# TensorE repeats an unread product at three of its waits in a gated attention and mixture-of-experts kernel

## The chip, the cores and the metric

The kernel runs on one core of one Trainium2 chip. The metric is the device time of one execution in microseconds (us). Below, TensorE is PE in the profile, VectorE is DVE, ScalarE is ACT, GpSimd is POOL, SyncE is SP; PEld is the loading of weights into TensorE's array, which is listed apart from its matmuls.

## What is computed

Input x is 8 batches of 512 tokens of 128 features, all f32. With `xn` the layer norm of x:

```
s = attention(xn)      # 8 heads of 16; out1 - lam * out2; layer norm; times Wo, plus bo
g = silu(ffn(xn))      # 8 experts of width 512; every token goes to experts h and h+1, h from its first two features
out = x + s * g
```

The attention applies a softmax over 512 keys in each of 64 head-and-batch pairs. Each expert is `relu(x @ W1 + b1) @ W2 + b2`, and the two experts of a token are averaged.

## The kernel before, in words

**The schedule.** Function `schedule` (L76) gives every step of the work a due time by hand and sorts the steps. Each engine then runs through the same sorted list and issues its own share of every step, so the order of steps on each engine is fixed when the program is built; semaphores hold an engine until what it needs is there. The step kinds that matter here are `invert`, `turn_tile`, `hidden`, `turn_o`, `turn_z`, `project_o` and `finish`.

**The routing.** VectorE finds for each token which slot of which expert's tiles it takes (`route`, L692 to L764). It and GpSimd then build 32 one-hot matrices `at_row` (`find_rows`, L381 to L386), in four groups of eight; groups 2 and 3 are GpSimd's (`POOL_ROWS`). TensorE's step `invert` (L1084 to L1096) waits for `token_ready` (L756) and then, group by group, for the matrices, and sums 32 products into one bank of PSUM: the token number of every slot. VectorE turns that into the indices `inverse` (L902 to L904). GpSimd then gathers the 128 rows of the first expert tile with an indirect DMA (`load_tile`, L537), and SP loads that tile's pair of experts' weights (L462).

**An expert tile.** There are 39. For each, TensorE transposes the gathered rows (`turn_tile`, L1097 to L1101), VectorE copies them out (L921), TensorE multiplies by the two experts' W1 (`hidden`, L1110), ScalarE and VectorE apply the bias and the maximum (L647, L928), TensorE multiplies by both W2 (`down`, L1125), VectorE adds a bias (L937) and GpSimd scatters the result (L571). Before the first tile's transpose TensorE's list has the first five scores and the transposes of batch 1 (L982); behind it come two scores, the first half of `hidden` of tile 0, a score, and a projection of batch 1 (L996).

**Attention.** For each of 256 blocks of 128 queries by 512 keys TensorE makes scores (L1015), VectorE takes their row maximum (L822), TensorE makes them again with the maximum subtracted (L1044, 24 blocks later), ScalarE takes the exponential (L628) and TensorE multiplies by the values (L1056). After two groups of 16 blocks a batch is turned (`turn_o`, L1064), normed on VectorE and GpSimd (L869 to L880 and L560 to L563), turned again (`turn_z`, L1066 to L1071), multiplied by Wo (`project_o`, L1076) and given its bias (L889).

**The end.** The last batch's `turn_o`, norm, `turn_z` and `project_o` come one after the other, with nothing else left in TensorE's list. Beside them VectorE and GpSimd do the `finish` of the batches (L378 and L379: times the gate, plus x), and SP stores the results.

**PSUM.** There are eight banks: two for scores, two for `exp_bank`, one for the product with the values, three in a ring. `exp_bank[0]` is first written when the 24th block of attention is due, and is no longer read once the last exponential is taken.

Of the kernel before, what the change touches and what calls it, by code (L numbers as in the profile page):

```python
# [11 lines left out]
P = 128  # L12
# [53 lines left out]
DVE_FINISH = tuple(b for b in range(B) if b not in POOL_FINISH)  # L66
FINISH_AT = (8.1, 8.2, 12.1, 12.2, 14.5, 8.1, 8.2, 18)
ROW_GROUPS = 4
RING = 3
DRAIN = NT * HEADS - LAG  # L70
WB = 3
# [71 lines left out]
def gated_attention_moe(nc, x, wq, bq, wk, bk, wv, bv, wo, bo, lq1, lk1, lq2, lk2,  # L143
# [19 lines left out]
    with ctx:  # L163
# [779 lines left out]
        def _(pe):  # L943
# [8 lines left out]
            for s, use in uses.items():  # L952
# [16 lines left out]
                    "hidden": lambda: (hid_ready[s[2]], s[1] + 1),  # L969
                }[kind]()  # L970

            w2_of = {}
            pe.wait_ge(consts_ready, 1)
            for s in steps:
# [32 lines left out]
                elif kind == "score":  # L1007
                    n = s[1]
                    b, col = divmod(n, HEADS * C)
                    hh, c = divmod(col, C)  # L1010
                    if col == 0:
                        pe.wait_ge(stacked[b % STK], 12 * 16 * (b // STK + 1))
                    if n >= 2:
                        pe.wait_ge(max_taken, n - 1)
                    t.matmul(score_bank[n % 2][:, :], qs[0:MAX_ROW, b % STK, hh, c * P:(c + 1) * P],  # L1015
                             ks[0:MAX_ROW, b % STK, hh, :], start=True, stop=True).then_inc(score_filled, 1)
                elif kind == "turn_max":
                    grp = s[1]
                    pe.wait_ge(max_split, grp + 1)
                    free(uses[s])  # L1020
                    t.transpose(shared[0:PARTS * 16, 0:P // 2].bitcast(BF16),
                                max_parts[:, grp % 2, :, :].rearrange("p j n -> p (j n)"),
                                ident_bf[:, :]).then_inc(shared_filled, 1)
                elif kind == "b1":
                    pe.wait_ge(b1_loaded, 16)
                    free(uses[s])
                    t.transpose(shared[:, 0:EXP * FC], b1_rows[:, :], ident[0:EXP * FC, 0:EXP * FC]).then_inc(shared_filled, 1)
                elif kind == "exp":
                    n = s[1]
                    b, r = divmod(n, HEADS * C)  # L1030
                    g2, r = divmod(r, C * HALF)
                    kc, i = divmod(r, HALF)
                    hh = g2 * HALF + i
                    if n % 16 == 0:
                        pe.wait_ge(max_stacked, 16 * (n // 16 + 1))
                        if n == 0:
                            pe.wait_ge(ones_stacked, 16 * STK)
                    if n >= DRAIN + 4:
                        pe.wait_ge(exp_done, n - 3)
                    elif n >= DRAIN + 2:  # L1040
                        pe.wait_ge(max_taken, n - DRAIN + NT * HEADS - 3)
                    elif n >= 2:
                        pe.wait_ge(exp_done, n - 1)
                    t.matmul(exp_banks[n][:, :], ks[0:KROWS, b % STK, hh, kc * P:(kc + 1) * P],  # L1044
                             qs[0:KROWS, b % STK, hh, :], start=True, stop=True).then_inc(exp_filled, 1)
                elif kind == "pv":
                    n4 = s[1]
                    grp, kc = divmod(n4, C)
                    b = grp // 2
                    pe.wait_ge(exp_done, 4 * n4 + 4)  # L1050
                    if n4 % (2 * C) == 0:
                        pe.wait_ge(va_ready, b + 1)
                    if kc == 0 and grp >= 1:
                        pe.wait_ge(o_copied, grp)
                    for i in range(HALF):
                        last = t.matmul(pv_bank[VW * i:VW * (i + 1), :], va[:, b % 2, kc, i, :],  # L1056
                                        probs[:, (4 * n4 + i) % PR, :], start=(kc == 0), stop=(kc == C - 1))
                    last.then_inc(pv_done, 1)
                elif kind == "turn_o":
                    grp = s[1]  # L1060
                    pe.wait_ge(o_copied, grp + 1)
                    free(uses[s])
                    for c in range(C):
                        last = t.transpose(shared[:, c * P:(c + 1) * P], oT[:, grp % 2, c * P:(c + 1) * P], ident[:, :])  # L1064
                    last.then_inc(shared_filled, 1)
                elif kind == "turn_z":  # L1066
                    pe.wait_ge(z_ready, s[1] + 1)
                    free(uses[s])
                    for c in range(C):
                        last = t.transpose(shared[:, c * P:(c + 1) * P], z[:, c, :], ident[:, :])  # L1070
                    last.then_inc(shared_filled, 1)  # L1071
                elif kind == "project_o":
                    pe.wait_ge(zT_ready, s[1] + 1)
                    free(uses[s])
                    for c in range(C):
                        last = t.matmul(shared[:, c * D:(c + 1) * D], zT[:, c * P:(c + 1) * P], wo_eff[:, :],  # L1076
                                        start=True, stop=True)
                    last.then_inc(shared_filled, 1)
                elif kind == "route" and s[1] == 1:
                    pe.wait_ge(count_ready, 1)  # L1080
                    free(uses[s])
                    t.matmul(shared[:, 0:EXP], before[:, :], count[:, :], start=True, stop=True)
                    t.matmul(shared[:, EXP:2 * EXP], ones[:, :], count[:, :], start=True, stop=True).then_inc(shared_filled, 1)
                elif kind == "invert":  # L1084
                    pe.wait_ge(token_ready, 1)
                    free(uses[s])
                    for q in range(ROW_GROUPS):
                        if q in POOL_ROWS:
                            pe.wait_ge(pool_row_ready, POOL_ROWS.index(q) + 1)
                        else:  # L1090
                            pe.wait_ge(at_row_ready, q + 1)
                        for tok in range(NT // ROW_GROUPS * q, NT // ROW_GROUPS * (q + 1)):
                            last = t.matmul(shared[:, 0:2 * FT], at_row[:, tok, :],
                                            token[:, tok, :, :].rearrange("p k f -> p (k f)"),
                                            start=(tok == 0), stop=(tok == NT - 1))
                    last.then_inc(shared_filled, 1)  # L1096
                elif kind == "turn_tile":  # L1097
                    f = s[1]
                    pe.wait_ge(tile_loaded[f % XS], 16 * (f // XS + 1))
                    free(uses[s])  # L1100
                    t.transpose(shared[:, 0:P], xs[:, f % XS, :], ident[:, :]).then_inc(shared_filled, 1)  # L1101
                elif kind == "hidden":
                    f, j = s[1:]
                    if j == 0:
                        pe.wait_ge(pair_loaded[f % WB], 16 * (f // WB + 1))
                        pe.wait_ge(xsT_ready, f + 1)
                    free(uses[s])
                    for c in range(FC):
                        o = j * TW + T_W1 + c * P
                        last = t.matmul(shared[:, c * P:(c + 1) * P], pair[:, f % WB, o:o + P], xsT[:, f % 2, :],  # L1110
                                        start=True, stop=True)
                    last.then_inc(shared_filled, 1)
                    if j == 1:
                        w2_of[f] = pe.snap(pe.value_load(texp[0:1, f:f + 1], min_val=0, max_val=EXP - 1) * FF)
                elif kind in ("down_first", "down"):
                    f = s[1]
                    half = int(kind == "down")
                    ks_of = range(FC * half, FC * (half + 1))
                    if f == 0 and half == 0:
                        pe.wait_ge(w2_loaded, 16 * (EXP + 1))  # L1120
                    pe.wait_ge(hid_ready[half], f + 1)
                    if half == 0:
                        free(uses[s])
                    for k in ks_of:
                        last = t.matmul(shared[:, 0:D], hT[:, f % 2, k, :], w2_sb[:, bass.ds(w2_of[f] + k * D, D)],  # L1125
                                        start=(k == 0), stop=(k == 2 * FC - 1))
                    if half == 1:
                        last.then_inc(shared_filled, 1)
# [27 lines left out]
```

## Time and profile before

| What | us |
|---|---|
| median of 3 runs | 479.77 |
| lowest and highest of them | 478.22, 480.86 |
| time of the profiled execution | 483.15 |
| its span, first to last instruction | 481.4 |
| TensorE busy in the span | 401.0 |
| VectorE busy | 336.4 |
| ScalarE busy | 227.8 |
| GpSimd busy | 149.3 |

The profiled execution is one more execution than the three timed. Its span leaves out 1.75 us that lie around the instructions. Times in the rows below count from the start of the span. Each matmul of f32 operands with 128 contraction rows is listed as two instructions, a transpose as one. The page's slices and the windows carry the clock that the throttle granted TensorE, 1.00 for 2.4 GHz and 0.50 for 1.2 GHz.

### The profile page before, as it was taken

The page shows a single profiled execution, that of the slowest core. Times are in us where ns is not written, and L with a number is a line of the kernel's source. Part 1 is how long each engine was busy: PE and PEld are TensorE (multiplying, and loading weights), DVE is VectorE, ACT ScalarE, POOL GpSimd, SP SyncE. Part 2 cuts the span into 40 slices and gives each one's busy share as a digit, 9 for nine tenths or more (in the row PEclk, how much of TensorE's full clock was granted, in tenths as well). Part 3 has the DMA queues.
Part 4 walks back from the last instruction along what each step waited for, and adds up shares of the span by engine and source line. Part 5 has one row for each costly group of instructions (what it writes and reads, how often), then busy time and mean ns, then how long its engine had stood idle before and what let it go on. Part 6 is the DMA issues. An engine that isn't in the chain of part 4 may idle for free.

```text
span 481.4 us, 8538 instructions
## 1 busy us (share of the span) xinstructions
PE 401.0 (83%) x2654; PEld 249.7 (52%) x2654; DVE 336.4 (70%) x893; ACT 227.8 (47%) x490; POOL 149.3 (31%) x186
## 2 busy tenths in 40 slices
PE   0301779999889999999989999999899999988932
PEld 0101457666555757565646656665666665622302
DVE  5586688766757776877677777768586767775357
ACT  2620122555544655465535545455456454544860
POOL 4349413134214331433232412333162133000132
PEclk9999999999999999999999999999999999997985
DMA  6999457143572139124914267313919431650004
GB/s 213 351 154 247 175 83 198 64 169 65 86 202 78 63 72 225 75 99 101 173 59 189 45 93 195 133 38 65 229 30 184 145 115 18 235 166 17 3 22 153
DMA packets 37838, 60.48 MB, mean 126 GB/s; under 512 B 6362, under 2 KB 25283, under 8 KB 37795
## 3 DMA queue, kind: packets, MB, share of 16 engines
q1 hardware_dynamic: 34099, 54.64, 42.5%
q0 software_dynamic: 2496, 5.12, 5.0%
q8 instruction: 23, 0.38, 0.4%
q10 hardware_dynamic: 1200, 0.18, 0.2%
q14 instruction: 20, 0.16, 0.2%
HBM read 14.60 MB, written 6.75 MB: 44 GB/s over the span
## 4 chain that ended last, share of the span: by engine, by line
PE 60%; DVE 13%; DMA 7%; issue 6%; ACT 4%; POOL 4%; SPq 3%; ACTq 1%; DVEq 0%; POOLq 0%
PE ring L1110 12%; PE pv_bank L1056 11%; PE score L1015 10%; PE ring L1125 9%; PE exp L1044 8%; DMA pair<-table 4%; DVE neg_max L822 3%; POOL pair L385 3%; PE ring L996 2%; PE ring L1076 2%; DMA qs<-max_rows 2%; DVE hT L928 1%; SPq L417 1%; PE ring L1064 1%; DVE stats_o L869 1%
## 5 line engine op out<-in xcount | busy, mean ns | idle before, releaser
L628 ACT ACTIVATE probs<-exp 128x512 f32<-128x512 f32 x244 | 141.1, 600 | 129.3 <-PE exp L1044 125.6
L822 DVE TENSOR_REDUCE neg_max<-score 128x1 f32<-128x512 f32 x256 | 170.0, 684 | 39.8 <-PE score L1015 38.3
L1015 PE MATMUL score<-ks,qs 96*128 96x512 bf16 x256 | 100.2, 395 | 12.5 <-DVE neg_max L822 12.0
L571 POOL DMA_INDIRECT y_rows<-y_sb,y_row x39 | 39.2, 1004 | 198.5 <-DVE y_sb L937 198.2
L1044 PE MATMUL exp<-qs,ks 99*128 99x512 bf16 x244 | 93.4, 387 | 4.0 <-DMA qs<-max_rows 2.5
L1110 PEld LDWEIGHTS ring<-xsT,pair 128*128 128x128 f32 x624 | 80.1, 193 | 19.2 <-issue 8.2
L1110 PE MATMUL ring<-xsT,pair 128*128 128x128 f32 x624 | 85.0, 280 | 4.5 <-DMA pair<-table 4.0
L647 ACT ACTIVATE hT<-ring,pair 128x128 f32<-128x128 f32 x156 | 44.6, 369 | 72.9 <-PE ring L1110 65.0
L1125 PE MATMUL ring<-w_sb,hT 128*128 x624 | 77.7, 277 | 1.4 <-DVE hT L928 1.4
L1125 PEld LDWEIGHTS ring<-w_sb,hT 128*128 128x128 f32 x624 | 74.7, 192 | 7.5 <-issue 3.3
L1056 PE MATMUL pv_bank<-probs,va 128*32 128x512 f32 x512 | 69.1, 612 | 0.8 <-ACT probs L628 0.7
L1015 PEld LDWEIGHTS score<-ks,qs 96*128 96x128 bf16 x256 | 26.6, 104 | 61.5 <-DVE neg_max L822 34.7
L928 DVE TENSOR_SCALAR hT<-ring,pair 128x128 f32<-128x128 f32 x156 | 43.8, 342 | 5.0 <-PE ring L1110 4.8
L537 POOL DMA_INDIRECT xs<-xn_rows,inverse x39 | 38.6, 989 | 11.2 <-issue 10.1
L1044 PEld LDWEIGHTS exp<-qs,ks 99*128 99x128 bf16 x244 | 24.1, 99 | 24.4 <-ACT probs L628 15.1
L937 DVE TENSOR_TENSOR y_sb<-ring,pair 128x128 f32<-128x128 f32 x39 | 11.2, 288 | 23.0 <-PE ring L1125 22.7
L560 POOL TENSOR_SCALAR var_eps_o<-mv_o 128x4 f32<-128x4 f32 x8 | 2.5, 307 | 70.5 <-DVE mv_o L872 70.5
L1056 PEld LDWEIGHTS pv_bank<-probs,va 128*32 128x32 f32 x512 | 10.1, 108 | 21.2 <-issue 15.9
L799 DVE SCALAR_TENSOR_TENSOR rest<-ring,qk_bias,parts 128x512 f32<-128x512 f32 x16 | 11.9, 749 | 11.2 <-ACT parts L617 11.2
L996 PE MATMUL ring<-xT,wqk 128*128 128x512 f32 x32 | 18.4, 665 | 0.8 <-ACT xT L599 0.8
L617 ACT ACTIVATE parts<-ring,qk_bias 128x512 bf16<-128x512 f32 x16 | 10.9, 688 | 16.6 <-PE ring L996 14.4
L921 DVE COPY xsT<-ring 128x128 f32<-128x128 f32 x39 | 11.1, 285 | 9.0 <-issue 4.7
(144 smaller groups left out, 337.1 us busy)
## 6 DMA issues: line engine op xcount, KB each, us to landing
pair<-table SPq DMA_DIRECT2D x39, 644.0 KB
qs<-parts SPq DMA_DIRECT2D x48, 128.0 KB
ks<-parts SPq DMA_DIRECT2D x48, 128.0 KB
w_sb<-in_L_ffn_W_dram SPq DMA_DIRECT2D x9, 256.0 KB, 6.0
s_sb<-_attn_hidden_states_dram SPq DMA_DIRECT2D x8, 256.0 KB, 5.5
table<-in_L_ffn_W_dram SPq DMA_DIRECT2D x2, 1024.0 KB, 10.9
xn_rows<-xn SPq DMA_DIRECT2D x8, 256.0 KB
table<-_attn_hidden_states_dram SPq DMA_DIRECT2D x8, 256.0 KB, 5.4
```

What stands on the lines that cost most here:

```text
L537: pool.indirect_dma_start(xs[:, f % XS, :], None, xn_rows, bass.IndirectOffsetOnAxis(ap=inverse[:, f:f + 1], axis=0)).then_inc(tile_loaded ...
L571: pool.indirect_dma_start(y_rows, bass.IndirectOffsetOnAxis(ap=y_row[:, f:f + 1], axis=0), y_sb[:, f % YB, :], None).then_inc(y_stored[f % ...
L628: a.activation(probs[:, n % PR, :], exp_banks[n][:, :], ACT.Exp, scale=SCALE).then_inc(exp_done, 1)
L647: last = a.activation(hT[:, f % 2, c, :], shared[:, c * P:(c + 1) * P], ACT.Relu, bias=pair[:, f % WB, T_B1 + c:T_B1 + c + 1])
L822: v.tensor_reduce(neg_max[:, b % 2, col:col + 1], score_bank[n % 2][:, :], AX.X, ALU.max, negate=True).then_inc(max_taken, 1)
L928: last = v.tensor_scalar(hT[:, f % 2, FC + c, :], shared[:, c * P:(c + 1) * P], pair[:, f % WB, TW + T_B1 + c:TW + T_B1 + c + 1], 0.0, ALU ...
L996: t.matmul(shared[:, :], wqk[:, i, :], xT[:, b % 2, :], start=True, stop=True).then_inc(shared_filled, 1)
L1015: t.matmul(score_bank[n % 2][:, :], qs[0:MAX_ROW, b % STK, hh, c * P:(c + 1) * P], ks[0:MAX_ROW, b % STK, hh, :], start=True, stop=True).t ...
L1044: t.matmul(exp_banks[n][:, :], ks[0:KROWS, b % STK, hh, kc * P:(kc + 1) * P], qs[0:KROWS, b % STK, hh, :], start=True, stop=True).then_inc ...
L1056: last = t.matmul(pv_bank[VW * i:VW * (i + 1), :], va[:, b % 2, kc, i, :], probs[:, (4 * n4 + i) % PR, :], start=(kc == 0), stop=(kc == C ...
L1110: last = t.matmul(shared[:, c * P:(c + 1) * P], pair[:, f % WB, o:o + P], xsT[:, f % 2, :], start=True, stop=True)
L1125: last = t.matmul(shared[:, 0:D], hT[:, f % 2, k, :], w2_sb[:, bass.ds(w2_of[f] + k * D, D)], start=(k == 0), stop=(k == 2 * FC - 1))
```

## The change

A helper `idle_products` is added to TensorE's program. It multiplies the f32 identity by itself, 128 by 128 by 128, into the first 128 columns of `exp_bank[0]`, as often as it is told, with no wait and no semaphore increment; nobody reads the result. It is called 12 times over in `invert`, after the wait for `token_ready` and ahead of the waits for the four groups of `at_row`; 6 times over in `turn_tile` of tile 0, ahead of the wait for the gathered rows, and behind all that stands earlier in TensorE's list; and 18 times over in `turn_z` of batch 7, ahead of the wait for `z_ready`.

```diff
+IDLE_INVERT, IDLE_FIRST, IDLE_LAST = 12, 6, 18
...
+            def idle_products(bank, count):
+
+                for _ in range(count):
+                    t.matmul(bank[:, 0:P], ident[:, :], ident[:, :], start=True, stop=True)
+
...
                 elif kind == "turn_z":
+                    if s[1] == B - 1:
+                        idle_products(exp_bank[0], IDLE_LAST)
                     pe.wait_ge(z_ready, s[1] + 1)
                     free(uses[s])
...
                 elif kind == "invert":
                     pe.wait_ge(token_ready, 1)
                     free(uses[s])
+                    idle_products(exp_bank[0], IDLE_INVERT)
                     for q in range(ROW_GROUPS):
...
                 elif kind == "turn_tile":
                     f = s[1]
+                    if f == 0:
+                        idle_products(exp_bank[0], IDLE_FIRST)
                     pe.wait_ge(tile_loaded[f % XS], 16 * (f // XS + 1))
                     free(uses[s])
                     t.transpose(shared[:, 0:P], xs[:, f % XS, :], ident[:, :]).then_inc(shared_filled, 1)
```

## Rows read from the trace of the kernel before

**Rows 1.** Windows: busy time of each engine by stage, then granted clock, DMA share, GB/s

```profile
60.00:75.00 15.00, 11.30 (x79) 8.98 (x77) 13.47 (x39) 3.62 (x9) 2.58 (x3) 1.00 0.56 91
...
130.00:425.00 295.00, 284.68 (x1968) 184.15 (x1967) 212.57 (x548) 151.81 (x333) 88.09 (x104) 1.00 0.47 118
```

**Rows 2.** Chain of waits ahead of the inverse: start, us, what

```profile
36.32 12.32 POOL pair L385 x16
```

**Rows 3.** Timeline around the inverse: start, us, engine, line, what, idle before it

```profile
39.18 0.65 DVE L756 TENSOR_SCALAR pair<-hT,row_of 128x1248 bf16<-128x1248 bf16 x1
...
44.05 0.70 PE L1093 MATMUL ring<-pair 128*128 128x78 bf16 x8 [0.73 <-POOL pair L385]
...
48.59 2.35 POOL L528 TENSOR_TENSOR table<-table 128x1024 f32<-128x1024 f32 x1
...
48.69 0.70 PE L1093 MATMUL ring<-pair 128*128 128x78 bf16 x8 [3.94 <-POOL pair L385]
...
49.19 1.05 PE L1015 MATMUL score<-ks,qs 96*128 96x512 bf16 x2
...
49.70 1.28 DVE L904 CAST inverse<-hT 128x39 int32<-128x39 f32 x1
...
52.20 1.20 PE L1015 MATMUL score<-ks,qs 96*128 96x512 bf16 x2 [1.96 <-DVE neg_max L822]
```

**Rows 4.** Timeline around the first expert tile and the work behind it

```profile
53.60 0.61 PE L1015 MATMUL score<-ks,qs 96*128 96x512 bf16 x1 [0.19 <-DVE neg_max L822]
...
54.00 1.06 PE L982 MATMUL ring<-ident,xn 128*128 128x128 f32 x4
...
54.85 0.42 PE L1101 MATMUL ring<-ident,xs 128*128 128x128 f32 x1
...
56.05 1.78 PEld L1110 LDWEIGHTS ring<-xsT,pair 128*128 128x128 f32 x8 [0.84 <-DMA pair<-table]
56.09 2.05 PE L1110 MATMUL ring<-xsT,pair 128*128 128x128 f32 x8
...
57.92 0.63 PE L1015 MATMUL score<-ks,qs 96*128 96x512 bf16 x1
...
58.35 1.36 PE L996 MATMUL ring<-xT,wqk 128*128 128x512 f32 x2
...
59.55 1.05 PE L1110 MATMUL ring<-xsT,pair 128*128 128x128 f32 x8
...
60.44 0.60 PE L1015 MATMUL score<-ks,qs 96*128 96x512 bf16 x2
...
66.88 0.39 PE L1015 MATMUL score<-ks,qs 96*128 96x512 bf16 x1 [1.92 <-DVE neg_max L822]
```

**Rows 5.** Windows with the granted clock around two stops near the end

```profile
432.50:435.00 2.50, 0.16 (x2) 0.03 (x2) 1.02 (x2) 0.55 (x1) 0.00 (x0) 0.90 0.54 201
...
438.00:441.00 3.00, 3.00 (x13) 0.65 (x6) 1.11 (x2) 0.84 (x2) 0.00 (x0) 0.50 0.00 0
...
464.00:466.00 2.00, 0.00 (x0) 0.00 (x0) 1.93 (x8) 2.00 (x4) 1.30 (x2) 0.80 0.00 0
```

**Rows 6.** Timeline: TensorE's first matmul behind the first of them

```profile
434.97 0.61 PE L1044 MATMUL exp<-qs,ks 99*128 99x512 bf16 x1 [2.34 <-DMA qs<-max_rows]
```

**Rows 7.** Timeline of the end

```profile
461.80 0.66 PE L1064 MATMUL ring<-ident,oT 128*128 128x128 f32 x4 [0.72 <-ACT oT L635]
...
467.57 5.16 DVE L880 TENSOR_SCALAR z<-attn,rstd_o,shift_o 128x128 f32<-128x128 f32 x4 [0.41 <-POOL shift_o L563]
...
472.78 1.12 PE L1070 MATMUL ring<-ident,z 128*128 128x128 f32 x4 [10.33 <-DVE z L880]
...
474.58 2.08 PE L1076 MATMUL ring<-wo_eff,zT 128*128 128x128 f32 x8 [0.69 <-ACT zT L640]
```

**Rows 8.** Timeline: the same two steps of batch 6

```profile
449.96 0.60 PE L1070 MATMUL ring<-ident,z 128*128 128x128 f32 x4
...
452.15 1.06 PE L1076 MATMUL ring<-wo_eff,zT 128*128 128x128 f32 x8
```

## Prediction, made before the changed kernel was run

> **What bounds the kernel now.** I read the windows by stage first. From 130 to 425 us TensorE is busy 284.68 of 295 us [rows 1]: it sets the time there, and what reaches that stretch late stays late. From 60 to 75 it is VectorE (13.47 of 15), fed by TensorE. TensorE has long stops only before 54 us and after 462 us, which is where the products are put. They can pay in one way alone: by keeping TensorE's clock up, so that real work behind a stop runs at 2.4 GHz.
>
> So I read the clock next. Near the end it is written out: a mean of 0.90 over 432.5 to 435, which is 1.00 until 434.5 and 0.50 from there, 0.50 at 438 to 441, and a mean of 0.80 over 464 to 466, which puts the second fall at 465.2 [rows 5]. At the start the column says 1.00 all along, but the durations deny it: a lone score takes 0.61 to 0.63 us at 53.60 and 57.92, as at 434.97 where the clock is at 0.50 [rows 4, 6], while behind 59.55 it takes 0.39. Eight matmuls of `hidden` take 57.92 - 56.09 = 1.83 us to the next start, and 60.44 - 59.55 = 0.89 us one half tile later [rows 4]. So TensorE is at 1.2 GHz from the start until about 59 us, and at 2.4 GHz from there. It came up after running almost without a stop since 52.20.
>
> From these pairs I take one price for all three places. A product of 128 by 128 by 128 in f32 is two listed matmuls of the shape of `hidden`: 1.83 / 8 = 0.229 us each at the low level, 0.89 / 8 = 0.111 us at the high one. A product is 0.46 or 0.22 us.
>
> **Part 1, twelve products ahead of the inverse.** `token_ready` comes when VectorE's L756 ends, 39.83 us [rows 3]. At the low level 24 matmuls take 24 x 0.229 = 5.5 us, to 45.3. The first three groups of `at_row` are there by then (the third ran at 44.05), and their 24 matmuls take at most 3 x 0.70 = 2.1 us [rows 3], to 47.4. The fourth group is GpSimd's, whose 16 comparisons end at 36.32 + 12.32 = 48.64 [rows 2], and runs at 48.69 as before. Cost: nothing; the cover is GpSimd's 12.3 us, of which 1.2 us stay. Without it up to 5.5 us would be on the path.
>
> The clock may well come up during these 7 us of unbroken work. I give that no gain. The fourth group would take perhaps 0.3 us less, but VectorE's cast to `inverse` (1.28 us, to 50.98) ends just after GpSimd's L528 does (48.59 + 2.35 = 50.94) [rows 3]. The cast's length looks like a wait for that, and SP's and GpSimd's loads of tile 0 need `inverse` and the table. What matters is whether the clock lasts until 54 us. Behind 47.4 come a stop to 48.69, some 1.5 us of work to 50.24, a stop of 1.96 us to 52.20 [rows 3]. At the higher level the work parts shrink to less than that and the stops grow to about 2 us each. The clock fell at 434.5, 1.9 us after TensorE's last work at 434.97 - 2.34 = 432.63, in a single stop of 2.34 us [rows 5, 6]; it did not fall in one of 1.92 us before 66.88, with much work on both sides [rows 4]. Two stops of 2 us with 1 us of work between lie nearer to the first. I take it that the clock is low again at 52.
>
> **Part 2, six products ahead of the first tile.** They start when the four transposes have been issued, at 54.85, where tile 0's transpose ran before with no wait at all: the tile had landed. So this is no waiting place in the trace; they push real work back. At the low level 12 x 0.229 = 2.75 us, to 57.6. Behind them queue on TensorE the tile's transpose, two scores, `hidden` (for which the pair of weights landed only at about 56.05, a cover that is gone: it is there by then), a score and the projection L996; for them wait VectorE's copies and maxima, and ScalarE's parts.
>
> Of 2.75 us not all is lost. Before, TensorE was busy without a break from 54.85 to the rise at 59, all at the low level. If the clock still rises at 59, the 2.75 us of real work that the products displace now runs above it, in 2.75 / 2 = 1.37 us. **The net price is 2.75 - 1.37 = 1.4 us.** Bounds: nothing if VectorE's stretch behind it took it up (VectorE idles 1.18 us before L799, but for the projection's result, which itself comes later); 2.75 us if the rise moved back by as much. I take 1.4, since the products leave no stop in which the rise could be put off. From 60 us on the delay passes through: VectorE's busy stretch starts from the projection, and later TensorE is the bound [rows 1].
>
> **Part 3, eighteen products ahead of the last z.** TensorE is free at 462.46, behind L1064. At the high level 36 x 0.111 = 4.0 us, to 466.5; at the low level 36 x 0.229 = 8.2 us, to 470.7. The last piece of z ends at 467.57 + 5.16 = 472.73 [rows 7]. Cost: nothing, with 2 us of cover left even then. What it could give: L1070 took 1.12 us against 0.60 for batch 6, and L1076 2.08 against 1.06 [rows 7, 8], together 1.5 us, all on the path. But the products end 6.3 us before z is there. Before, the clock fell 2.7 us after TensorE's last work [rows 5, 7] and at 434.5 after 1.9 us; a stop of 6.3 us is far over both. So I take 0, the lower end, and keep -1.5 as the other.
>
> **Sum.** 0 + 1.4 + 0 = 1.4 us. Against the profiled execution's own time: 481.4 of span and 1.75 around it are 483.15, to 484.6. That execution lies 3.4 us over the median of 479.77, so on the median's side I forecast 479.77 + 1.4 = **481.2 us**. About 0.5% (2.4 us) is what a measurement of this kernel can tell from no change; my forecast is inside it.
>
> **Rivals.**
>
> 1. **The clock stays up from the inverse on.** For it: 7 us of unbroken work, more than came before the rise at 59. Against it: the two stops above. If it holds, the work between 54.0 and 59 halves. The transposes take 0.43 us, to 54.4; the products 12 x 0.111 = 1.33, to 55.8; the tile's transpose and two scores end at 56.3, `hidden` starts at 56.35 instead of 56.09, and with 0.89 + 0.22 + 0.86 us the projection is through at 58.4, instead of 58.35 + 1.36 = 59.7 [rows 4]: about 1.2 us gained. Time: 478.6. The Trainium skill (TensorE: Matmul & The Clock Gate, "Why this matters for your kernels") speaks for this case: short gaps between bursts leave the clock up, and only a longer idle stretch brings it back down. The fall inside a stop of 2.34 us [rows 6] does not sit well with it.
>
> 2. **The push is taken up.** Weights of tile 0 at 56.05 and VectorE's idle time before L799 are slack that I have counted as gone. Nothing is lost then: 479.8. Against it: TensorE itself had no idle time from 53.60 to 60 [rows 4].
>
> 3. **The products cost their full length (slower).** The place is the same, ahead of tile 0. If the rise comes later by as much as the products last, no displaced work is run at the high level and the price is 2.75 us; with a little knocked on in VectorE's full stretch, 482.6. This decides if the chip does not count these products as it counts real work: an identity times an identity is nearly all zeros. Rows 5 show only real data. The same would make parts 1 and 3 idle.
>
> 4. **The end runs at the high level.** z would have to be ready by about 469, or the clock to last 6 us unused. 481.2 - 1.5 = 479.7.
>
> That the change doesn't do what it says (the products skipped or merged) is hardly possible: each is an instruction in TensorE's list; then nothing changes, 479.8, which rival 2 covers.
>
> **How the numbers follow.** Forecast 0.60, rival 1 0.11, rival 2 0.10, rival 3 0.15, rival 4 0.04. Runs of one kernel spread by 1.3 us about the median (478.22 to 480.86), so each case gets about that. Range: down to 478.2, which takes in the larger part of rival 1 and all of 2 and 4, up to 483.3 for rival 3. Slower by over 0.5% means over 482.2: most of rival 3 and a sixth of the forecast, 0.20. Faster means under 477.4: rival 1 with a good run, or with rival 4, 0.06. The rest, 0.74, is within 0.5%.
>
> **What would show it.** Right: 24 matmuls of 0.23 us pitch from 39.9 on, the fourth group still at about 48.7; the lone scores at 52 to 53 still of 0.6 us; twelve matmuls between the transposes L982 and L1101, 2.7 us long; the projection L996 of batch 1 ending near 61.0 instead of 59.7; 36 matmuls at the end of 0.11 us pitch, then over 5 us of stop with a fall of the clock in it; L1070 at 1.1 and L1076 at 2.1 us again. Wrong: scores of 0.39 us at 53 (rival 1); L996 at its old time (rival 2) or past 62 (rival 3); L1076 at 1.06 us (rival 4). A fourth group later than 48.7 would upset part 1.

## The result, and the profile after

The changed kernel takes **485.66 us** (median of 4 runs, 484.13 to 488.67) against 480.31 before (4 runs): a ratio of 1.0108, 95% interval 1.006 to 1.0156. It is slower by 5.3 us where I had forecast 1.4. The ratios here and below leave out runs that lie more than 1.5% over the fastest of their kernel; where a kernel's own runs spread wider than that, the ratio is too kind to it, and the median over all its runs stands beside it.

The page of the changed kernel, its first lines, TensorE's slices and the queue of instruction loads:

```profile
span 482.4 us, 8682 instructions
...
PE 406.9 (84%) x2726; PEld 257.7 (53%) x2726; DVE 336.6 (70%) x893; ACT 227.5 (47%) x490; POOL 149.0 (31%) x186
...
PEclk9999799999999999999999999999999999998995
...
q8 instruction: 24, 0.39, 0.4%
```

There are 144 more instructions: 36 products, each two matmuls and two weight loads. Queue q8 has one packet more than before (23 then). Its packets are 0.39 MB / 24 = 16 KB each. I read past this line of the page; it turns out to be the one that matters most.

The front of the changed kernel in the timeline, TensorE alone (start, us; against [rows 3, 4]), and then three windows in which the clock shows (the third column from the end):

```profile
39.28 4.31 PE L976 MATMUL exp<-ident 128*128 128x128 f32 x24 [7.94 <-DVE pair L757]
43.42 1.05 PE L1102 MATMUL ring<-pair 128*128 128x78 bf16 x24
48.03 0.47 PE L1102 MATMUL ring<-pair 128*128 128x78 bf16 x8 [3.56 <-POOL pair L386]
51.54 1.20 PE L1021 MATMUL score<-ks,qs 96*128 96x512 bf16 x2 [2.61 <-DVE neg_max L823]
54.19 2.29 PE L976 MATMUL exp<-ident 128*128 128x128 f32 x12
56.31 0.27 PE L1112 MATMUL ring<-ident,xs 128*128 128x128 f32 x1
58.20 1.02 PE L1002 MATMUL ring<-xT,wqk 128*128 128x512 f32 x2
```

```profile
42.00:48.50 6.50, 2.94 (x46) 2.73 (x46) 1.09 (x3) 0.00 (x0) 6.50 (x12) 1.00 0.29 81
48.50:49.00 0.50, 0.43 (x2) 0.00 (x0) 0.43 (x2) 0.00 (x0) 0.50 (x1) 0.99 0.00 0
50.00:60.00 10.00, 8.27 (x42) 6.12 (x43) 6.90 (x15) 1.76 (x5) 2.45 (x3) 0.71 0.54 213
```

The twelve products do bring the clock up, at 42.2 us (the fourth group takes 0.47 us instead of 0.70), and it is down again at 49.0, before it could serve: the scores at 51.54 take 1.20 us for two, as before. A mean of 0.71 over 50 to 60 is 0.50 until 55.8. From the third score to the second `y_sb` of VectorE (the end of tile 1) this stage takes 21.81 us; before it took 21.64. All starts here lie about 0.6 us earlier than in the trace of before, and TensorE's first matmul, ahead of every product, does as well (10.71 against 11.39 us). In this execution the front costs 0.2 us.

The loss is behind it. TensorE's waits for the weights of a tile (in all, how many, the longest), before and after:

```profile
PE ring L1110 <- DMA pair<-table: 4.0, 3, 1.7
```

```profile
PE ring L1121 <- DMA pair<-table: 7.2, 5, 2.0
```

Between the second and the last `y_sb` the changed kernel takes 351.65 us, before 348.57. The delay does not grow evenly. It jumps by 2.1 us at tile 14, 1.3 at tile 25 and 0.7 at tile 30, each time at such a wait.

The two profiled executions are closer than the medians: 483.15 and 484.13 us, the slowest of the kernel before and the fastest of the changed one. Of the 3.1 us lost in the middle 1.6 are won back between the last `y_sb` and the last z, where the clock falls for 6.8 us before [rows 5] and for 3.4 us, at 438.1, in the changed kernel; 0.7 come from the earlier start.

The end, against [rows 7]:

```profile
463.29 4.18 PE L976 MATMUL exp<-ident 128*128 128x128 f32 x36
473.78 1.11 PE L1078 MATMUL ring<-ident,z 128*128 128x128 f32 x4 [6.31 <-DVE z L881]
475.58 2.07 PE L1084 MATMUL ring<-wo_eff,zT 128*128 128x128 f32 x8 [0.69 <-ACT zT L641]
```

From the first transpose of z to the end of the span it is 8.6 us in both. The eighteen products end at 467.5, TensorE stops for 6.31 us, and both steps run at the low level, as before.

### The profile page after: what moved, and what is told of

Its sections match the earlier page's. It is cut to its first block, busy times and chain, and to the rows that moved or that the text cites. A ratio compares the mean times of both kernels' runs of the same rounds, so it can differ in the third digit from the quotient of the medians.

```text
span 482.4 us, 8682 instructions
## 1 busy us (share of the span) xinstructions
PE 406.9 (84%) x2726; PEld 257.7 (53%) x2726; DVE 336.6 (70%) x893; ACT 227.5 (47%) x490; POOL 149.0 (31%) x186
## 4 chain that ended last, share of the span: by engine, by line
PE 56%; DVE 15%; DMA 10%; issue 6%; POOL 5%; SPq 4%; ACT 3%; DVEq 0%; ACTq 0%; POOLq 0%
PE ring L1121 11%; PE pv_bank L1062 10%; PE score L1021 9%; PE ring L1136 9%; PE exp L1050 7%; DMA pair<-table 7%; DVE neg_max L823 3%; POOL pair L386 2%; SPq L418 2%; PE ring L1002 2%; PE ring L1084 2%; DVE hT L929 1%; PE ring L1070 1%; DMA qs<-max_rows 1%; POOL rstd L515 1%
## 5 line engine op out<-in xcount | busy, mean ns | idle before, releaser
L1021 PE MATMUL score<-ks,qs 96*128 96x512 bf16 x256 | 98.3, 387 | 13.3 <-DVE neg_max L823 12.7
L1050 PE MATMUL exp<-qs,ks 99*128 99x512 bf16 x244 | 92.4, 383 | 2.8 <-DMA qs<-max_rows 1.8
```

## The experiments

**One place at a time.** The four kernels of this group ran on one chip, where before is 481.55 us.

```diff
+IDLE_INVERT, IDLE_FIRST, IDLE_LAST = 12, 6, 18    # e1_all
+IDLE_INVERT, IDLE_FIRST, IDLE_LAST = 12, 0, 0     # e2_invert
+IDLE_INVERT, IDLE_FIRST, IDLE_LAST = 0, 6, 0      # e3_first
+IDLE_INVERT, IDLE_FIRST, IDLE_LAST = 0, 0, 18     # e4_last
```

> The changed kernel once more, all three places. Theory A (what I forecast, only the six products ahead of tile 0 cost): the loss lies ahead of 62 us, 1.4 to 2.75 us, so the median stays under 483.5. Theory B (the loss arises in the middle, where waits for the weights of a tile grew from 4.0 to 7.2 us in the one profile of the changed kernel): 484 to 487 again, with the front within 0.5 us of before and 3 us or more of added waits for pair<-table between 130 and 425 us. Theory C (chance between runs): 480 to 482.

> Only the twelve products ahead of the inverse; the other two counts are 0. Theory A: no change, 480.3, since GpSimd's comparisons cover them. Theory B: if anything that shifts the early steps brings the loss in the middle, part of it shows here, 482 or more; if it needs the shift at tile 0, no change. The profile should show the clock up at about 42 to 46 us and down again before 53.

> Only the six products ahead of the first tile. Theory A: this holds the whole loss, 1.4 to 2.75 us, and L996 of batch 1 ends over 1 us later than before. Theory B with the shift at tile 0: 484 or more, with longer waits for pair<-table. If both are wrong: 480.3.

> Only the eighteen products ahead of the last transposes of z. Theories A and B: no change, 480.3, the clock falls in the stop behind them and L1078 and L1084 of batch 7 take 1.1 and 2.1 us. Theory D (the length of the program itself costs, or the products slow what runs beside them at the end): 481 or more here.

| Kernel | median | over before | ratio, 95% interval |
|---|---|---|---|
| all three | 489.09 | +7.5 | 1.0155, 1.0114 to 1.0196 |
| inverse only | 486.21 | +4.7 | 1.0036, 0.9992 to 1.008 |
| first tile only | 484.12 | +2.6 | 1.0046, 1.0015 to 1.0077 |
| last z only | 480.83 | -0.7 | 0.9987, 0.9961 to 1.0012 |

The inverse's products, which my working covers fully, cost the most. Their runs spread from 479.55 to 491.98, and the interval of the ratio still touches 1; but seven of the twelve lie above every one of the 29 runs of before, whose highest is 485.06. Theory A is out. In the profile of that kernel the front is even shorter than before (20.87 us), and then come two long waits, each followed by a fall of the clock. Its waits for weights, and two windows behind the first of the two:

```profile
PE ring L1121 <- DMA pair<-table: 7.4, 3, 3.5
```

```profile
291.00:293.00 2.00, 1.29 (x8) 1.29 (x9) 0.00 (x0) 0.00 (x0) 0.00 (x0) 0.81 0.98 334
293.00:299.00 6.00, 6.00 (x27) 5.14 (x26) 2.60 (x7) 2.23 (x6) 0.00 (x0) 0.50 0.26 106
```

Behind the wait for tile 25 (2.3 us) TensorE works without a stop for 6 us at 1.2 GHz, which costs about 3 us on top of the wait. Only the last z, whose instructions stand behind all the tiles, costs nothing. So it matters where in TensorE's list the products are added, and not how long they run. That led to the instruction loads: in the traces the 16 KB packets of q8 come about every 18 us and, counted in TensorE's matmuls and weight loads, 251 to 257 instructions apart on average, and an added instruction moves all later ones earlier against the work. With the shift some of them fall just behind the issue of the weight loads that TensorE waits for.

**The same instructions where they cost no time, and a shift by a whole block.** On another chip; before is 481.06 us. The additions stand ahead of the wait for `count_ready`, where TensorE is idle from about 17 to 31 us:

```diff
                 elif kind == "route" and s[1] == 1:
+                    idle_products(exp_bank[0], PAD_PRODUCTS)
+                    for _ in range(PAD_SMALL):
+                        t.matmul(exp_bank[0][0:32, 0:16], ident_bf[:, 0:32], ident_bf[:, 0:16], start=True, stop=True)
                     pe.wait_ge(count_ready, 1)
...
+PAD_PRODUCTS, PAD_SMALL = 18, 0     # e5_pad_products, with 0, 0, 0 at the three places
+PAD_PRODUCTS, PAD_SMALL = 0, 92     # e6_all_block, with 12, 6, 18
+PAD_PRODUCTS, PAD_SMALL = 0, 128    # e7_pad_256, with 0, 0, 0
+PAD_PRODUCTS, PAD_SMALL = 0, 80     # e8_pad_160, with 0, 0, 0
```

> None of the three places; instead 18 of the same products (72 instructions, as many as the first two places add) where TensorE is idle between 18 and 31 us and where they change no later start. Theory E (a block of TensorE's own instructions, 16 KB = 256 instructions of 64 bytes, is fetched about every 17 us; the added instructions move these fetches onto the loads of expert weights that TensorE waits for, at tiles 14, 25 and 30): 484.5 to 488, with the front as before and waits for pair<-table of 6 us or more. Theory B' (it is the changed times of the early steps that shift the DMAs against each other): 481.5, waits of 4 us.

> The whole change, plus 92 tiny matmuls (184 instructions) in the idle stretch before 31 us, so that everything behind the first tile is moved by exactly one block of 256 instructions. Theory E: the fetches are back at their old places and the loss of the middle is gone: 481 to 483, which is the change's own price (0 to 1.4 us at the front). Theory B': 486 to 489 as before.

> The kernel before, plus 128 tiny matmuls (256 instructions, one block) in the same idle stretch. Control: theory E says 481.5, no change. Theory F (it is the number of added instructions that costs, wherever): 485 or more.

> The kernel before, plus 80 tiny matmuls (160 instructions). By the traces a shift of 16 to 96 instructions puts fetches into the flights of the late loads, and one of 100 to 230 keeps them out. Theory E: no slower than before, and faster by 1 to 3 us where the waits of tiles 9, 20 and 30 (1.7, 0.9 and 1.3 us in the trace of before) shrink: 478.5 to 481. Theories B' and F: 481.5 or more.

| Kernel | instructions ahead of the tiles | median | over before | ratio, 95% interval |
|---|---|---|---|---|
| 18 products early | +72 | 487.91 | +6.9 | 1.0169, 1.013 to 1.0209 |
| all, and one block | +256 | 483.84 | +2.8 | 1.0054, 1.0027 to 1.0081 |
| small ones only | +256 | 480.82 | -0.2 | 1.0003, 0.9979 to 1.0027 |
| small ones only | +160 | 482.46 | +1.4 | 1.0022, 0.9989 to 1.0055 |

Of the whole change with one block, one of the ten runs took 1023.34 us, for no reason that the record shows; without it the median is 483.61.

Eighteen products in an idle stretch, long done before anything needs TensorE, cost nearly as much as the whole change (6.9 and 7.5 us, on two chips). A full block of 256 costs nothing, and added to the whole change it takes back most of the loss. Theories B' and F are out. Tile 30 shows it best. First the issue of its load and the matmul that waits for it, then the queues in the DMA view of just this stretch. In the kernel with 18 early products:

```profile
334.43 0.54 SPq L464 DMA_DIRECT2D pair<-table  x1
...
342.61 1.65 PE L1125 MATMUL ring<-xsT,pair 128*128 128x128 f32 x6 [3.41 <-DMA pair<-table]
```

```profile
q1 hardware_dynamic: 1015, 1.45, 98.7%
q0 software_dynamic: 32, 0.07, 6.3%
q8 instruction: 1, 0.02, 1.2%
```

In the whole change shifted by one block:

```profile
335.68 0.54 SPq L464 DMA_DIRECT2D pair<-table  x1
...
340.82 1.16 PE L1125 MATMUL ring<-xsT,pair 128*128 128x128 f32 x8 [0.47 <-DMA pair<-table]
```

```profile
q1 hardware_dynamic: 597, 1.08, 98.6%
```

From issue to first matmul it is 8.2 us with a packet of q8 in the flight (1.4 us behind the issue) and 5.1 without; TensorE waits 3.41 or 0.47 us. In the trace of before there is none in tile 30's flight either, and the wait is 1.31. The other traces give the same order for this tile: 5.1 to 5.9 us in the twelve without a packet in the flight, 6.0 and 6.7 in the two with one 3.4 and 3.8 us behind the issue, 7.5 to 8.2 in the three with one 0.5 to 1.4 us behind it.

The order doesn't hold at every tile. At tile 14, where the changed kernel loses most, the flight takes 6.0 and 6.6 us with a packet 0.9 and 1.2 us behind the issue and 4.0 to 4.3 without; but in the trace of the changed kernel the packet comes 3.9 us behind and the flight takes 6.2, while packets at 3.7 and 4.0 us in two other traces leave it at 4.5 and 4.3. At tile 20 nearly every trace has a packet, and no such order shows.

The kernel with 160 was a miss: it was to be no slower than before, and its median is 1.4 us over, though the interval reaches down to 0.9989. It cleared tiles 14, 20, 25 and 30, and put a packet 2.2 us behind the issue for tile 33, which had never been late. Here it and, below it, the same tile with 256:

```profile
361.81 0.54 SPq L464 DMA_DIRECT2D pair<-table  x1
...
371.03 1.16 PE L1125 MATMUL ring<-xsT,pair 128*128 128x128 f32 x8 [3.17 <-DMA pair<-table]
```

```profile
362.19 0.54 SPq L464 DMA_DIRECT2D pair<-table  x1
...
368.18 1.07 PE L1125 MATMUL ring<-xsT,pair 128*128 128x128 f32 x8
```

My list of endangered tiles had been drawn from late loads alone. It should have had every tile whose load is needed within about 9 us of its issue. The miss itself is one more case of the same cause: one packet, a wait of 3.2 us.

**The inverse's own price, a shift without products, a better shift, and the end kept at the high level.** On a third chip; before is 480.95 us.

```diff
+IDLE = 12, 0, 0;  PAD_SMALL = 104    # e9_invert_block, 48 + 208 instructions
+IDLE = 0, 0, 0;   PAD_SMALL = 36     # e10_small_72
+IDLE = 0, 0, 0;   PAD_SMALL = 104    # e11_pad_208
+IDLE = 0, 0, 44;  PAD_SMALL = 0      # e12_last_44
```

> Only the twelve products ahead of the inverse (48 instructions) plus 104 tiny matmuls (208) in the idle stretch before 31 us: one block of 256 in all. Theory E: the 4.7 us that the twelve products cost alone are gone, 480.5 to 481.5, since GpSimd's comparisons cover them. Theory B' (the early steps' changed times): 484 or more, as for the products alone.

> The kernel before plus 36 tiny matmuls (72 instructions) in the idle stretch before 31 us, and no product at all. Theory E: as slow as with 18 products in that place (+6.9 us), so 486 or more, with waits for pair<-table of 6 us. Theory G (it is the products' own activity at about 20 us, through the clock, that costs later): 481, no change.

> The kernel before plus 104 tiny matmuls (208 instructions). With 160 the fetches missed the late loads of tiles 9 to 30 but one fell 2.2 us behind the issue of tile 33's load, which cost 3.2 us. With 208 that fetch comes about 1 us ahead of the issue, and no other one falls in the first 4 us of tiles 9, 14, 20, 25 or 30. Theory E: 479 to 481, a little faster than before. If where a fetch falls in a flight does not matter as I think: 482 or more.

> Only the products ahead of the last z, 44 of them in place of 18. At 0.224 us each they run from 462.4 to about 472.3, close up to z at 472.7, so the clock should still be high there. My part 3 priced this at -1.5 us: transposes of 0.60 us instead of 1.12, projection of 1.06 instead of 2.08, a stretch from the first transpose of z to the end of the span of 7.2 instead of 8.6 us, median 479.5 to 480. If the clock falls all the same, or the time behind the transposes does not depend on TensorE: 481 and 8.6 us.

| Kernel | median | over before | ratio, 95% interval |
|---|---|---|---|
| inverse, and one block | 481.39 | +0.4 | 1.0005, 0.9978 to 1.0032 |
| 72 small instructions | 487.89 | +6.9 | 1.0063, 1.0007 to 1.0118 |
| 208 small instructions | 481.48 | +0.5 | 0.9999, 0.9968 to 1.003 |
| 44 products ahead of the last z | 480.90 | 0.0 | 0.9993, 0.9964 to 1.0021 |

With the packets back in place the inverse's products cost nothing, as their cover says. And 36 tiny matmuls, 1.06 us of work in an idle stretch of 14, cost 6.9 us by the median; by the ratio it is less, but ten of their twelve runs lie above all 35 of before. No product is needed for the loss, and no clock brought up early: the rise comes at 57.6 us as in the kernel with 18 early products. The waits alone don't make it up. In this trace they sum to 6.5 us against 4.0 before, and behind two of them (tiles 14 and 30) the clock falls for 3.4 us each, which it does not do in the trace of before. The shift of 208 is as good as before and no better; its waits for weights sum to 4.0 us as before, with 1.88 at tile 9 where no packet of q8 is near. These waits have a cause of their own as well, which I did not look for.

The 44 products are the more instructive miss. TensorE and VectorE at the end of that kernel:

```profile
461.19 9.99 PE L977 MATMUL exp<-ident 128*128 128x128 f32 x88
471.72 0.66 PE L1079 MATMUL ring<-ident,z 128*128 128x128 f32 x4 [0.54 <-DVE z L882]
473.06 1.16 PE L1085 MATMUL ring<-wo_eff,zT 128*128 128x128 f32 x8 [0.69 <-ACT zT L642]
474.95 0.69 DVE L381 TENSOR_TENSOR s_sb<-s_sb,table 128x512 f32<-128x512 f32 x1
475.56 0.68 DVE L891 TENSOR_TENSOR s_sb<-ring,bo_eff 128x512 f32<-128x512 f32 x1
```

The clock stayed up, and both steps take little more than half their time: the projection is done at 474.22. But VectorE takes it only at 475.56, when the last `finish` of the batches ahead of it in its list is through. It has been at them without a break since z. From the first transpose of z to the end of the span it is 8.54 us instead of 8.61. In the trace of before the two ran level, the projection's end at 474.58 + 2.08 = 476.66 and VectorE free at 476.71, and the chain of waits named TensorE alone.

**What the six products cost by themselves.** Open was why the whole change with its packets in place still lost 2.8 us, where its front shows 1.2 (22.84 us from the third score to the second `y_sb`, against 21.62 with 256 small instructions). On the first chip again; before is 480.09 us.

```diff
+IDLE = 0, 6, 0;    PAD_SMALL = 116    # e13_first_block, 24 + 232 instructions
+IDLE = 12, 6, 18;  PAD_SMALL = 92     # e14_all_block_again
+IDLE = 0, 0, 0;    PAD_SMALL = 128    # e15_pad_256_again
```

> Only the six products ahead of tile 0 (24 instructions), plus 116 tiny matmuls (232): one block in all, so the fetches keep their places. The front by itself costs what its stage shows, 22.84 instead of 21.62 us from the third score to the second y_sb: median 1.2 us over before. If the 2.6 us that the products cost alone come from something behind the front as well, 2.6 us again, with a stage behind it that is longer.

> The whole change with the fetches at their old places, once more: the first time it was 2.8 us over before. If the front is all of it: 1.2 us over, within an interval that reaches from 0.3 to 2.5 us. If there is more: 2.8 us again.

> The same 256 instructions ahead with no product at all, as the control of the two others on the same chip: no change from before, within 0.5 us.

| Kernel | median | over before | ratio, 95% interval |
|---|---|---|---|
| first tile, and one block | 483.11 | +3.0 | 1.005, 1.0026 to 1.0074 |
| all, and one block | 483.85 | +3.8 | 1.0064, 1.0039 to 1.009 |
| 256 small instructions | 480.79 | +0.7 | 1.0009, 0.9983 to 1.0035 |

The price repeats: about 3 us, and the six products alone have it. In these traces none of it is in the front. The stage from the third score to the second `y_sb` takes 21.7 and 21.6 us, against 22.0 in the control. Of the 2.75 us between the spans of the first and the third kernel, 1.6 open at one place, behind the wait of 1.6 us for tile 9's weights that all of them have. This is the same stretch in the first and in the third kernel:

```profile
137.40:144.40 7.00, 7.00 (x32) 6.02 (x31) 2.72 (x7) 2.23 (x6) 0.00 (x0) 0.51 0.46 172
```

```profile
137.40:144.40 7.00, 6.99 (x42) 5.44 (x42) 2.98 (x9) 2.82 (x7) 0.00 (x0) 0.76 0.52 189
```

A granted clock of 0.51 against 0.76: the low level lasts about 6.8 and 3.4 us, and the delay grows by 1.6 us. Another 1.2 us open between the last `y_sb` and the last z, where the clock falls for 3.4 us at 437.9 in the first kernel and not at all in the third. In the trace of before it does not fall at tile 9, and it does not in the first trace of the whole change with one block either, the same kernel as the second of this group. So a kernel does not always have the fall; it differs from run to run.

The runs' own clocks bear this out. In some runs the record of the clock begins only at its rise, at 45 to 59 us in the traces, and their granted clock is 0.969 or more, against 0.95 or less where the record begins at 16 to 20 us. Of twelve such runs of the first two kernels ten have 0.969 to 0.973 and take 483.05 to 485.15 us; the other two have 0.979 and 0.981 and take 480.50 and 479.67. Before, beside them, has thirteen, none below 0.976. A share lower by 0.006 is 2 x 0.006 x 482 = 5.8 us more at the low level, and at half speed 2.9 us of time. But the kernel before has the slower kind too: six of seventeen when the first group ran, on the same chip (0.971 to 0.975, 483.33 to 485.06 us), and eight of sixteen on the chip of the third group. The six products seem to make it more frequent; they bring in nothing that was not there.

## Why the prediction was wrong

**Bounds and prices.** The reading of the clock held; where the record begins early it is written out, as low from 20.9 to 58.5 us with 256 small instructions. The price of a matmul was a little high at the low level, 0.213 us instead of 0.229 (twelve take 2.56 us where the clock is low all through, from 54.14 to 56.70 with the six products alone). At the high one 36 take 4.18 us, where I had 4.0.

**Part 1, "Cost: nothing; the cover is GpSimd's 12.3 us".** This is the step that failed most. As engine time it is right: with a whole block's shift the twelve products cost 0.4 us, inside the interval, and the fourth group never ran later. But I costed an instruction by its duration alone. The 48 instructions moved every later load of TensorE's instructions by 48 places against the work, and with that packets of 16 KB onto the flights of weight loads (2.0 us behind the issue at tile 25 and 1.3 at tile 30, with waits of 2.3 and 3.5 us and a fall of the clock behind each): +4.7 us by the median. I had a rival for products not done, and none for what an added instruction does to those behind it. The page showed the queue.

**The clock behind the inverse.** I took it to fall between 47.4 and 52, and it did, at 49.0 in the changed kernel. Rival 1 is out. The rule that short gaps leave the clock up (the Trainium skill, TensorE: Matmul & The Clock Gate, "Why this matters for your kernels") is not what this case's traces show: ahead of the fall at 49.0 lies a stop of 3.56 us, which might still count as long, but in the kernel of six products and one block one of 1.62 us, with full work on both sides, was followed by the low level at 137.6, and in the changed kernel one of 1.64 us, ended at 436.9, by the low level at 438.1. My own sign, that the clock had stayed up through the stop of 1.92 us before 66.88, was no sign either: with six products alone the same stop of 1.92 us is followed by the low level at 67.9, for 3.4 us.

**Part 2, "the net price is 2.75 - 1.37 = 1.4 us".** A push is there, but it is not where most of the loss lies, so this step failed as well. The push is largest where the products run at the low level all through: 22.84 us for the stage in two kernels, against 21.62 in the control; 0.9 us of the difference is there when the projection ends, the rest behind the fall of the clock at 68 us that both have. Where the rise comes during the products the stage takes 21.64 to 21.97 us. But it varies by itself, from 20.96 to 21.97 us over the nine traces without products at the first two places, with the time at which the clock rises; the six traces with the six products average 22.1, those nine 21.4. So the push is worth about 0.7 us, half of what I had, and the median price is 2.6 to 3.8 us in four comparisons. What I had no term for is more time at the low level far behind the products, at tile 9's wait and near 437 us, which makes up the difference between the two spans and parts the slower runs from the others. Why six products at 54 us make a fall at 137 longer or more frequent is not settled. It was not tried. Rival 3 had the right size (2.75 us) by the wrong cause: the clock rises at 42.2 us with nothing but such products run since 39.28, so the chip does count them.

**Part 3, cost nothing.** Right: -0.7 us for the eighteen alone, 0.9961 to 1.0012. The reason for no gain was right as well (a stop of 6.31 us, low level behind it). The upper end was not: "together 1.5 us, all on the path" is 0.07 us. I took the chain of waits at its word and did not ask what VectorE had in its list. Rival 4 could not have paid, and did not when the clock was kept up.

**Sum.** My range ended at 483.3; the slower side had 0.20. The misplaced instruction loads, with the falls of the clock behind the waits that they make, are worth about 4 to 5 us (7.5 for the whole change against 2.8 and 3.8 with one block), the six products about 3, the rest nothing. Both parts were missing from my sum, which was made of engine time at the three places alone. The parts do not simply add up: 72 instructions without any push cost 6.9 us, since where a packet falls in a flight depends on both.

## What to carry to other kernels

An instruction that costs no engine time is not free in a long unrolled program: it moves all later instruction loads of its engine against the data loads, so compare a small change with the same number of instructions placed elsewhere, and with a whole block of 256, before reading its time as its own. A kernel in which loads land just in time can lose more than 1% to such a shift alone: this one lost 6.9 of 481 us to 72 small instructions. Where a short wait is followed by a fall of the clock, its price is more than its length: read the granted clock behind every wait, not the row of waits alone. Warming an engine's clock pays only if it is kept up until the work comes and if that work, and not the list of the engine behind it, sets the end.

## What the runs showed of the hardware

- TensorE's instructions come in packets of 16 KB by a DMA queue of its own (q8). The packet count goes from 23 to 24 with 256 instructions more, while the other queue of this kind, q14, stays at 20 there, and the packets are 251 to 257 of TensorE's instructions apart on average (single gaps are 190 to 311 in the trace of before). The Trainium skill gives the same size (Advanced Engine Details and Errata, "ISA Cache": a line of 16 KB holds 256 instructions).
- One such packet, 1.4 to 2.2 us behind the issue of a load of 644 KB, made that load about 3 us later (tiles 30 and 33); 5.9 us behind, as at tile 25 in the trace of before, it did nothing. At tile 14 a packet 3.7 to 4.0 us behind was followed by a late load in one trace of three. The packet itself takes 0.9 to 1.9 us. Why the load is late by more than that is open.
- TensorE's clock can fall behind a single wait of 1.6 us in the middle of full work (tile 9) and then stay low for 3.4 or 6.8 us, or not fall at all, in executions of the same kernel. From the ninth to the twelfth `y_sb` the traces take 30.3 to 31.0 us without the fall, 32.3 and 32.5 with the shorter and 34.0 with the longer one. So it costs as much as the wait or twice as much, and is not in any row of waits.
